# A fused GNN, Mamba and mixture-of-experts kernel: blocks chosen by the eight largest keys, logits folded by the transposing product, sums written as integers

## The chip, the cores and the metric

One core of one Trainium2 chip. The metric is the device time of one execution in microseconds (us); the time before is the median of three runs. The trace is that of one profiled execution with its own time.

## The reference

8192 rows of 128 channels pass a graph convolution and a Mamba block, then a feed-forward layer in which each row is sent to one of eight experts:

```
h = relu(adj @ layernorm(x) @ gcn_w + gcn_b); h = layernorm(h) * ln_g + ln_b
xc, z = split(h @ w_in); u = silu(conv4(xc) + conv_b); dt, B, C = from u @ w_xp
hst = exp(dt * A) * hst + dt * B * u          # a scan over the 8192 rows, 16 states
x = x + ((hst @ C + u * D) * silu(z)) @ w_out
H = gelu(layernorm(x) @ W1 + b1); probs = softmax(H @ Wg + bg)
e = argmax(probs); x = x + probs[e] * (H @ Wd[e] + bd[e])
```

## The kernel before

The rows are cut into 16 tiles of 512. Each engine (TensorE: PE, VectorE: DVE, ScalarE: ACT, GpSimd: POOL, SyncE: SP) runs its own hand-written program of bodies i = -2 to 15, each of 16 slots s. In body i, DVE scans the 16 states of tile i, one state in each slot (L984), with the product for the next state (L1057) and the running sum (L1027) beside it, POOL multiplies the states by C (L506), PE streams the adjacency product of tile i+2 (L1197), and the expert work of tile i-1 is strewn over the slots. The order on each engine is the order of the code; engines meet at semaphores that count finished steps.

Three small pieces of DVE work in each body belong to the experts.

- `logits_below_max` (slot 12): ACT has copied the partial logits from PSUM to `front_b` (L564), where channel 32k+e holds the part of expert e from quarter k of the hidden units; PE has transposed the four blocks of 128 columns into `ps_y` (L1175). DVE adds the four quarters (L943), adds the bias `bg` (L945), takes the largest (L948) and subtracts it (L950). `probability` (slot 14) picks the expert.
- `destinations` (slot 0, in the last body also slot 9): PE has ranked the rows of a tile by expert; DVE computes for each row its place in the bins in DRAM, as a float sum (L900), casts it (L902), masks it to an integer (L904) and moves the expert's `tail` on (L906). POOL then scatters the rows into the bins.
- `control` (slot 1 of bodies 4 to 15): of 32 candidate blocks (eight experts, four blocks each) those that are full (`has`) are numbered by a scan along the row (L843, L846); four masks of 32 say which candidate has number 1, 2, 3 and 4 (`chosen`, L848), and a product and a sum (L852, L856) give the four block starts, cast to integers (L861) and split into expert (`owner`) and row (`row_at`). SP reads those numbers into registers and loads the four blocks and the weights of their experts; PE, ACT and DVE then run the batch.

After the last tile five more batches empty the bins. Their `control` has the flag `flush`, and then also finds which rows are missing (L868 to L874). Batch 0's stands in slot 9 of body 15; those of batches 1 to 4 (`choose`) come behind the bodies. After them the dense computation of the last tile and the late batches run.

Between DVE instructions that depend on each other stands a wait on the step counters `ctrl_step`, `flush_step`, `gate_step` and `dest_step`.

Of the kernel before, what the change touches and what calls it, by code (L numbers as in the profile page):

```python
# [37 lines left out]
AX = mybir.AxisListType.X  # L38
EXP_LN_SET = "natural_log_exp_and_others"
# [11 lines left out]
def gnn_mamba_moe(nc, x_rows, x_cols, adj, vecs, consts, sel, gcn_w, w_in, w_xp, w_dt, w_out, W1, Wg, Wd, bd, out):  # L51
# [12 lines left out]
    with ExitStack() as ctx:  # L64
# [20 lines left out]
        eps_col = sb("eps_col", [P, 1])  # L85

# [56 lines left out]
        dest_f = sb("dest_f", [P, BLOCKS])  # L143
# [6 lines left out]
        turn = sb("turn", [P, PICKS, EXPERTS * PICKS])  # L150
        unit_row = sb("unit_row", [P, EXPERTS * PICKS])

        has = sb("has", [P, EXPERTS, PICKS])
        order = sb("order", [P, EXPERTS, PICKS])
# [5 lines left out]
        first_f = sb("first_f", [P, 2, PICKS])  # L160
# [73 lines left out]
        def cells(ap):  # L234
            return ap.rearrange("p b c -> p (b c)")
# [46 lines left out]
        gate_step, expo_ready, rank_done = sem("gate_step", 9), sem("expo_ready"), sem("rank_done")  # L282
        dest_step, scat_in = sem("dest_step", 6), sem("scat_in", 16 * BLOCKS)

        ctrl_step, flush_step = sem("ctrl_step", 13), sem("flush_step", 17)
# [60 lines left out]
        def _(sp):  # L346
# [36 lines left out]
            def body(i, p, adjacency, front, mamba, ffn, scatter, batch, late):  # L383
# [6 lines left out]
                for s in range(SLOTS):  # L390
# [20 lines left out]
                    if s == 9 and batch:  # L411
                        for n in range(AREAS):
                            sp.wait_ge(zero_in[n], 16 * PARTS)
                        c.wait(ctrl_step, -4, 13)
# [19 lines left out]
            def late_rows(f):  # L434
                sp.wait_ge(flush_step, 17 * f + 17)
# [24 lines left out]
        def _(pool):  # L460
# [7 lines left out]
            constant(turn[:], [[1, PICKS], [0, EXPERTS * PICKS]], 1, 0)  # L468
# [15 lines left out]
            def body(i, p, adjacency, front, mamba, ffn, scatter, batch, late):  # L484
# [3 lines left out]
                for s in range(SLOTS):  # L488
                    if late and s in OUT_SLOTS:
                        c.wait(o_ready, -5, PICKS + 1)  # L490
                    if scatter and s == 1:
                        if i - 2 < AREAS:
                            pool.wait_ge(zero_in[i - 2], 16 * PARTS)
                        c.wait(dest_step, -2, 6)
                        c.wait(xn_ready, -2, BLOCKS)
                        c.wait(id_step, -2, 1)
                    if fast and s == 10:
                        c.wait(dest_step, -1, 6)
# [32 lines left out]
        def _(act):  # L531
# [26 lines left out]
            act.wait_ge(start_a, 2)  # L558

            def logit_columns(c, front):  # L560
# [3 lines left out]
                nc.scalar.copy(front_b[:], ps_y[:, 0]).then_inc(cols_ready, 1)  # L564

            def body(i, p, adjacency, front, mamba, ffn, scatter, batch, late):
# [32 lines left out]
                for s in range(SLOTS):  # L599
# [105 lines left out]
                    if ffn and s == (7 if fast else 13):  # L705
                        c.wait(gate_step, -1, 4)
# [56 lines left out]
            c.wait(gate_step, -1, 4)  # L763
# [12 lines left out]
        def _(dve):  # L776
# [4 lines left out]
            nc.vector.memset(unit_row[:], 1.0).then_inc(start_v, 1)  # L781
            nc.vector.memset(ones[:], float(EXPERTS)).then_inc(start_v, 1)
            dve.wait_ge(start_c, 8)
# [30 lines left out]

            rest = H[0:EXPERTS, 0, 0:P]
# [8 lines left out]
            dve.wait_ge(start_v, 9)  # L824
            dve.wait_ge(part_step, 6)

            def control(c, d, r, flush):
# [3 lines left out]
                def after(n):  # L831
                    if flush:
                        dve.wait_ge(flush_step, 17 * d + n)
                    else:
# [28 lines left out]
                nc.vector.tensor_scalar(owner[:, r], row_at[:, r], EXPERTS - 1, None, ALU.bitwise_and  # L863
                                        ).then_inc(mark, 1)
                nc.vector.tensor_scalar(row_at[:, r], row_at[:, r], SPACE - 1, None, ALU.bitwise_and
                                        ).then_inc(mark, 1)
                if flush:
                    nc.vector.tensor_tensor(left[:], over_picks(tail[:]), cand[:], ALU.subtract).then_inc(mark, 1)  # L868
                    after(14)
                    nc.vector.tensor_tensor(weigh[:], chosen[:], over_turns(left[:]), ALU.mult).then_inc(mark, 1)  # L870
                    after(15)
                    nc.vector.reduce_sum(first_f[:, 1], weigh[:], AX).then_inc(mark, 1)
                    after(16)
                    nc.vector.tensor_scalar(absent[:, r - 2], first_f[:, 1], need[:, 0:1], float(1 << 30), ALU.is_lt,  # L874
# [16 lines left out]
            def destinations(c, d):  # L891
# [46 lines left out]
            def logits_below_max(c):  # L938
# [3 lines left out]
                quarters = ps_y[:, 0].rearrange("p (b k e) -> p b e k", b=BLOCKS, k=4)[:, :, 0:EXPERTS]  # L942
# [476 lines left out]
```

## Time and profile before

| | |
|---|---|
| median of three runs | 1755.98 us (1751.51 to 1758.42) |
| the profiled execution | 1760.01 us, of it 1758.2 us from the first to the last instruction (the span) |
| busy in the span | DVE 1537.9 us (87%), PE 1434.7 (82%), ACT 883.6 (50%), POOL 790.0 (45%) |
| mean granted TensorE clock | 0.911 of full speed |

The times in the rows below are us from the span's start; a bracket at the end of a row of the timeline says how long the engine stood idle before it and whose work ended that. Where one row begins 0.2 us after another, that is all the time that the first one costs its engine: an instruction's own length overlaps the next where no wait stands between them.

### The profile page before, as it was taken

What the parts mean: (1) busy time and instruction counts of PE and PEld (TensorE: products, weight loads), DVE (VectorE), ACT (ScalarE), POOL (GpSimd) and SP (SyncE); (2) the same over time, 40 slices, a digit from 0 to 9 for tenths busy, and PEclk for the clock granted to TensorE, in tenths of its full rate; (3) what the DMA queues carried; (4) which work ended last, traced back from release to release, by engine and by line L of the source; (5) the groups of instructions that cost most, each with busy time, mean ns of one, the idle gap of its engine ahead of it and who ended that gap; (6) DMA issues with size and microseconds to landing.
All of it is one profiled execution on the core that took longest, in us unless ns stands there. A gap on an engine that the chain in (4) does not pass through costs nothing. (4 is left out here: it accounts for less than half of the span.)

```text
span 1758.2 us, 15991 instructions
## 1 busy us (share of the span) xinstructions
PE 1434.7 (82%) x4051; PEld 658.9 (37%) x4051; DVE 1537.9 (87%) x2022; ACT 883.6 (50%) x1574; POOL 790.0 (45%) x396
## 2 busy tenths in 40 slices
PE   5998898888889898988989888889898894523487
PEld 2433333333334444444443434444444332221354
DVE  8057969898999999999999999999999999999842
ACT  3143445363636547473827465554737383734441
POOL 0013333443435355555545545555555454545622
PEclk9999999999999998999999999999899996665699
DMA  8888899899998888888888888878888884424350
GB/s 308 280 287 289 318 336 323 315 338 363 329 350 301 296 298 298 299 302 293 289 290 296 280 303 288 301 278 304 303 298 287 286 297 164 142 90 147 108 160 16
DMA packets 157806, 476.92 MB, mean 271 GB/s; under 512 B 19693, under 2 KB 41760, under 8 KB 157586
## 3 DMA queue, kind: packets, MB, share of 16 engines
q1 hardware_dynamic: 114098, 324.56, 52.9%
q10 hardware_dynamic: 38560, 139.48, 23.0%
q0 software_dynamic: 5056, 11.87, 1.8%
q8 instruction: 32, 0.52, 0.1%
q14 instruction: 60, 0.49, 0.1%
HBM read 445.75 MB, written 32.97 MB: 272 GB/s over the span
## 5 line engine op out<-in xcount | busy, mean ns | idle before, releaser
L1197 PE MATMUL ps_adj<-ring,nodes 128*128 128x512 f32 x2048 | 969.5, 621 | 117.1 <-DMA ring<-adj 58.5
L506 POOL TENSOR_TENSOR h_c<-hidden,bc_ring 128x1024 f32<-128x1024 f32 x256 | 602.1, 2352 | 876.4 <-DVE inject L1057 676.5
L984 DVE TENSOR_TENSOR_SCAN hidden<-decay,state,inject 128x512 f32<-128x512 f32 x512 | 627.6, 1267 | 53.8 <-ACT decay L584 30.8
L1197 PEld LDWEIGHTS ps_adj<-ring,nodes 128*128 128x128 f32 x2048 | 396.0, 199 | 642.4 <-issue 462.4
L584 ACT ACTIVATE decay<-dt_sb,negA 128x512 f32<-128x512 f32 x512 | 339.5, 712 | 9.5 <-DVE dt_sb L1011 7.5
L1057 DVE TENSOR_TENSOR inject<-dtu_sb,bc_ring 128x1024 f32<-128x1024 f32 x256 | 314.3, 1228 | 26.5 <-DMA bc_ring<-bc_dram 21.9
L577 ACT COPY state<-hidden 128x2 f32<-128x2 f32 x255 | 49.1, 193 | 496.0 <-DVE hidden L984 495.5
L1027 DVE TENSOR_TENSOR y_sum<-y_sum,h_c 128x1024 f32<-128x1024 f32 x224 | 273.6, 1221 | 7.7 <-POOL h_c L506 4.6
L480 POOL DMA_INDIRECT out<-o_sb,out_at x68 | 98.8, 1453 | 78.5 <-DVE o_sb L887 64.4
L475 POOL DMA_INDIRECT bins<-rec,dest x60 | 87.8, 1464 | 10.2 <-issue 9.3
L1124 PE MATMUL ps_f<-u_sb,wxp_sb 128*128 128x512 f32 x64 | 44.0, 825 | 42.4 <-ACT u_sb L663 42.4
L1124 PE MATMUL ps_e<-bt_sb,w_sb 128*128 128x512 f32 x112 | 61.0, 672 | 16.1 <-ACT H L714 10.7
L1124 PE MATMUL ps_e<-wd_ring,H 128*128 128x128 f32 x448 | 61.5, 293 | 14.1 <-ACT H L714 12.9
L1124 PE MATMUL ps_f<-front_a,win_sb 128*128 128x512 f32 x128 | 65.4, 637 | 4.0 <-DVE front_a L1007 2.8
L1036 DVE SCALAR_TENSOR_TENSOR u_sb<-conv_in,vec_sb,u_sb 128x512 f32<-128x512 f32 x96 | 65.0, 745 | 3.5 <-ACT u_sb L649 3.5
L1124 PEld LDWEIGHTS ps_e<-wd_ring,H 128*128 128x128 f32 x448 | 58.6, 202 | 25.1 <-ACT H L714 20.2
L1124 PE MATMUL ps_y<-wout_sb,soft 128*128 128x128 f32 x256 | 35.4, 297 | 19.2 <-DVE soft L936 19.2
L1124 PEld LDWEIGHTS ps_y<-wout_sb,soft 128*128 128x128 f32 x256 | 35.0, 213 | 28.1 <-DVE soft L936 20.8
L1007 DVE TENSOR_TENSOR front_a<-ps_f,front_b 128x512 f32<-128x512 f32 x16 | 10.9, 683 | 38.1 <-ACT front_b L619 38.1
L1124 PEld LDWEIGHTS ps_e<-bt_sb,w_sb 128*128 128x128 f32 x112 | 22.2, 212 | 51.3 <-issue 24.8
L605 ACT COPY front_a<-ps_adj 128x512 f32<-128x512 f32 x16 | 9.3, 581 | 63.4 <-PE ps_adj L1197 63.4
L1165 PE MATMUL ps_y<-const_sb,rec 128*128 128x128 f32 x64 | 11.2, 302 | 36.4 <-ACT rec L630 35.4
(203 smaller groups left out, 1271.1 us busy)
## 6 DMA issues: line engine op xcount, KB each, us to landing
ring<-adj SPq DMA_DIRECT2D x512, 512.0 KB, 5.9
bc_ring<-bc_dram ACTq DMA_DIRECT2D x256, 512.0 KB, 6.1
wd_ring<-wd_rows SPq DMA_DIRECT2D x64, 288.0 KB, 3.2
bins<-nodes SPq DMA_DIRECT2D x32, 516.0 KB, 8.0
got<-bins SPq DMA_DIRECT2D x60, 129.0 KB, 2.5
nodes<-x_rows ACTq DMA_DIRECT2D x8, 512.0 KB, 12.7
x_tile<-x_rows SPq DMA_DIRECT2D x16, 256.0 KB, 7.6
wd_rows<-Wd SPq DMA_DIRECT2D x8, 256.0 KB, 7.2
```

The lines of the kernel that those rows point to most:

```text
L475: nc.gpsimd.indirect_dma_start(out=bins.ap(), out_offset=bass.IndirectOffsetOnAxis(ap=dest[:, b:b + 1], axis=0), in_=rec[:, q, b], in_offs ...
L480: nc.gpsimd.indirect_dma_start(out=out, out_offset=bass.IndirectOffsetOnAxis(ap=out_at[:, r, j:j + 1], axis=0), in_=o_sb[:, r, j], in_offs ...
L506: nc.gpsimd.tensor_tensor(h_c[:, s % 2], hidden[:, s % 2], over_halves(bc_ring[:, s % BC_RING, 1]), ALU.mult).then_inc(hc_ready, 1)
L577: nc.scalar.copy(state[:, :, t:t + 1], hidden[:, t % 2, :, T - 1:T]).then_inc(state_ready, 1)
L584: exp = nc.scalar.activation(decay[:, t % 2, h], dt_sb[:, p if d == 0 else q, h], ACT.Exp, scale=negA[:, h, t:t + 1])
L984: scan = nc.vector.tensor_tensor_scan(hidden[:, s % 2, h], decay[:, s % 2, h], inject[:, h], state[:, h, s:s + 1], ALU.mult, ALU.add)
L1027: nc.vector.tensor_tensor(y_sum[:], y_sum[:], h_c[:, (s - 1) % 2], ALU.add).then_inc(y_step, 1)
L1036: nc.vector.scalar_tensor_tensor(out=u_sb[:, h], in0=conv_in[:, h, k:k + T], scalar=vec("conv_w", TAPS * h + k), in1=u_sb[:, h], op0=ALU.m ...
L1057: nc.vector.tensor_tensor(inject[:], dtu_sb[:], over_halves(bc_ring[:, t % BC_RING, 0]), ALU.mult).then_inc(inject_ready, 1)
L1124: last = nc.tensor.matmul(dst, stationary, moving, start=(n == 0), stop=(n == len(pairs) - 1))
L1165: last = nc.tensor.transpose(ps_y[:, 0, b * P:(b + 1) * P], xn_rows[:, q, b], ident)
L1197: last = nc.tensor.matmul(ps_adj[:, 0], nodes[:, m], ring[:, g % RING, m % GROUP], start=(m == 0), stop=(m == J - 1))
```

## The change

- `control`: a key for each candidate, 2^20 for a full block minus the candidate's start; one `max` instruction gives the eight largest keys of each row in falling order, so the smallest starts first. The fourth key is the threshold for `left`, and the first four, taken from 2^20 and written as integers, are the block starts. The scan, its mask, and in the non-flush form the four masks, their product and their sum go. The flush form makes the masks from the keys, later, and for the missing rows alone.
- `logits_below_max`: PE multiplies each block of `front_b` by a matrix `fold` [128, 8] that adds the four quarters, in place of the transpose; ACT's copy adds the bias (`Identity` with `bg_col`). DVE's two instructions for the quarters and the bias go, and the other two read PSUM.
- `destinations`: the sum writes integers, and the cast goes.
- At the start DVE makes `fold` and `bg_col` with three small instructions, and one memset and one iota go; ACT's bodies wait for them.

```diff
 def control(c, d, r, flush):
     ...
     after(2)
-    nc.vector.tensor_tensor_scan(cells(order[:]), unit_row[:], cells(has[:]), 0.0, ALU.mult, ALU.add
-                                 ).then_inc(mark, 1)
+    nc.vector.scalar_tensor_tensor(out=key[:], in0=has[:], scalar=float(BASE), in1=cand[:],
+                                   op0=ALU.mult, op1=ALU.subtract).then_inc(mark, 1)
     after(3)
-    nc.vector.tensor_tensor(order[:], order[:], has[:], ALU.mult).then_inc(mark, 1)
+    nc.vector.max(best[:], cells(key[:])).then_inc(mark, 1)
     after(4)
-    nc.vector.tensor_tensor(chosen[:], over_turns(order[:]), turn[:], ALU.is_equal).then_inc(mark, 1)
-    nc.vector.scalar_tensor_tensor(out=left[:], in0=order[:], scalar=float(PICKS), in1=has[:],
-                                   op0=ALU.is_le, op1=ALU.mult).then_inc(mark, 1)
+    nc.vector.tensor_scalar(left[:], key[:], best[:, PICKS - 1:PICKS], None, ALU.is_ge).then_inc(mark, 1)
+    nc.vector.tensor_scalar(row_at[:, r], best[:, 0:PICKS], -1.0, float(BASE), ALU.mult, ALU.add
+                            ).then_inc(mark, 1)
     after(5)
-    nc.vector.tensor_tensor(weigh[:], chosen[:], over_turns(cand[:]), ALU.mult).then_inc(mark, 1)
+    nc.vector.reduce_sum(taken[:], left[:], AX).then_inc(mark, 1)
     after(6)
-    nc.vector.reduce_sum(taken[:], left[:], AX).then_inc(mark, 1)
+    nc.vector.tensor_scalar(owner[:, r], row_at[:, r], EXPERTS - 1, None, ALU.bitwise_and
+                            ).then_inc(mark, 1)
     after(7)
-    nc.vector.reduce_sum(first_f[:, 0], weigh[:], AX).then_inc(mark, 1)
-    after(8)
     nc.vector.scalar_tensor_tensor(out=head[:], ...)
-    after(9)
-    nc.vector.tensor_copy(row_at[:, r], first_f[:, 0]).then_inc(mark, 1)
-    after(11)
-    nc.vector.tensor_scalar(owner[:, r], ...)
     nc.vector.tensor_scalar(row_at[:, r], row_at[:, r], SPACE - 1, None, ALU.bitwise_and
                             ).then_inc(mark, 1)
     if flush:
         nc.vector.tensor_tensor(left[:], over_picks(tail[:]), cand[:], ALU.subtract).then_inc(mark, 1)
+        nc.vector.tensor_tensor(chosen[:], over_turns(key[:]), best[:, 0:PICKS]..., ALU.is_equal).then_inc(mark, 1)
         ...
 def destinations(c, d):
     ...
-    nc.vector.reduce_sum(dest_f[:], place[:], AX).then_inc(dest_step, 1)
+    nc.vector.reduce_sum(dest[:], place[:], AX).then_inc(dest_step, 1)
     c.wait(dest_step, d, 3)
-    nc.vector.tensor_copy(dest[:], dest_f[:]).then_inc(dest_step, 1)
-    c.wait(dest_step, d, 4)
 def logits_below_max(c):
     ...
-    nc.vector.reduce_sum(logit[:], quarters, AX).then_inc(gate_step, 1)
+    nc.vector.reduce_max(top[:, 0], sums_of, AX).then_inc(gate_step, 1)
     c.wait(gate_step, -1, 1)
-    nc.vector.tensor_tensor(logit[:], logit[:], over_blocks(vec("bg", 0, EXPERTS)), ALU.add
+    nc.vector.tensor_tensor(logit[:], sums_of, over_experts(top[:, 0]), ALU.subtract
                             ).then_inc(gate_step, 1)
-    c.wait(gate_step, -1, 2)
-    nc.vector.reduce_max(top[:, 0], logit[:], AX).then_inc(gate_step, 1)
-    c.wait(gate_step, -1, 3)
-    nc.vector.tensor_tensor(logit[:], logit[:], over_experts(top[:, 0]), ALU.subtract
-                            ).then_inc(gate_step, 1)
 def logit_columns(c, front):                      # ACT
-    nc.scalar.copy(front_b[:], ps_y[:, 0]).then_inc(cols_ready, 1)
+    nc.scalar.activation(front_b[:], ps_y[:, 0], ACT.Identity, bias=bg_col[:, 0:1]).then_inc(cols_ready, 1)
 def logits():                                     # PE
-    last = nc.tensor.transpose(ps_y[:, 0, b * P:(b + 1) * P], front_b[:, b * P:(b + 1) * P], ident)
+    last = product(ps_y[:, 0, b * EXPERTS:(b + 1) * EXPERTS],
+                   [(front_b[:, b * P:(b + 1) * P], fold[:])])
 # DVE, at the start
+nc.vector.reduce_sum(fold[:], ident.rearrange("p (k e) -> p e k", k=4)[:, 0:EXPERTS], AX).then_inc(start_v, 1)
+nc.vector.tensor_tensor(expo[:, 0], ident[:, 0:EXPERTS], vec("bg", 0, EXPERTS), ALU.mult).then_inc(start_v, 1)
+dve.wait_ge(start_v, 10)
+nc.vector.reduce_sum(bg_col[:], expo[:, 0], AX).then_inc(start_v, 1)
```

DVE's program in slot 1 of a body before, from the test for full blocks to the masked row numbers:

```order
L839 SCALAR_TENSOR_TENSOR has<-cand,tail 128x32
L843 SCALAR_TENSOR_TENSOR order<-unit_row,has 128x32
L846 TENSOR_TENSOR order<-order,has 128x32
L848 TENSOR_TENSOR chosen<-order,turn 128x128
L849 SCALAR_TENSOR_TENSOR left<-order,has 128x32
L852 TENSOR_TENSOR weigh<-chosen,cand 128x128
L854 TENSOR_REDUCE taken<-left 128x8
L856 TENSOR_REDUCE first_f<-weigh 128x4
L858 SCALAR_TENSOR_TENSOR head<-taken,head 128x8
L861 CAST row_at<-first_f 128x4
L863 TENSOR_SCALAR owner<-row_at 128x4
L865 TENSOR_SCALAR row_at<-row_at 128x4
```

The same stretch of the change, on DVE, in the same slot:

```order
L842 SCALAR_TENSOR_TENSOR has<-cand,tail 128x32
L846 SCALAR_TENSOR_TENSOR key<-has,cand 128x32
L849 MAX best<-key 128x8
L851 TENSOR_SCALAR left<-key,best 128x32
L852 TENSOR_SCALAR row_at<-best 128x4
L855 TENSOR_REDUCE taken<-left 128x8
L857 TENSOR_SCALAR owner<-row_at 128x4
L860 SCALAR_TENSOR_TENSOR head<-taken,head 128x8
L862 TENSOR_SCALAR row_at<-row_at 128x4
```

Twelve instructions have become nine, the three 128 elements wide among them gone, and nothing else has moved across them: `cand` still stands ahead of the piece, and the running sum and the next state's product behind it.

DVE's program around the logits of slot 12 before, between the running sum and the next scan:

```order
L1027 TENSOR_TENSOR y_sum<-y_sum,h_c 128x1024
L943 TENSOR_REDUCE logit<-ps_y 128x32
L945 TENSOR_TENSOR logit<-logit,vec_sb 128x32
L948 TENSOR_REDUCE top<-logit 128x4
L950 TENSOR_TENSOR logit<-logit,top 128x32
L1057 TENSOR_TENSOR inject<-dtu_sb,bc_ring 128x1024
```

And in the change:

```order
L1020 TENSOR_TENSOR y_sum<-y_sum,h_c 128x1024
L941 TENSOR_REDUCE top<-ps_y 128x4
L943 TENSOR_TENSOR logit<-ps_y,top 128x32
L1050 TENSOR_TENSOR inject<-dtu_sb,bc_ring 128x1024
L977 SCALAR_TENSOR_TENSOR hidden<-decay,state,inject 128x512 x2
```

Two of the four are gone, and the two that stay now take `ps_y` as their input.

## Rows read from the trace of the kernel before

**Rows 1.** Two stretches: length, busy us of each engine (instructions), clock, DMA share, GB/s

```profile
318.00:415.00 97.00, 80.60 (x202) 33.29 (x200) 89.00 (x101) 45.81 (x87) 43.71 (x20) 0.95 0.92 334
612.00:710.00 98.00, 88.49 (x252) 40.63 (x251) 94.75 (x122) 56.75 (x100) 50.36 (x24) 0.93 0.83 291
```

**Rows 2.** What DVE waited for from 552 to 1618: us, times, longest

```profile
DVE inject L1057 <- DMA bc_ring<-bc_dram: 12.9, 10, 3.4
DVE hidden L984 <- ACT decay L584: 1.8, 3, 0.8
```

**Rows 3.** What DVE waited for from 115 to 552

```profile
DVE hidden L984 <- ACT decay L584: 29.8, 9, 10.0
```

**Rows 4.** Timeline of DVE: the control of body 4, start, us, line, operation

```profile
519.27 0.17 DVE L837 TENSOR_TENSOR cand<-head,offset 128x32 f32<-128x32 f32 x1
519.47 0.19 DVE L839 SCALAR_TENSOR_TENSOR has<-cand,tail 128x32 f32<-128x32 f32 x1
...
520.40 0.18 DVE L849 SCALAR_TENSOR_TENSOR left<-order,has 128x32 f32<-128x32 f32 x1
520.51 0.29 DVE L852 TENSOR_TENSOR weigh<-chosen,cand 128x128 f32<-128x128 f32 x1
...
521.44 0.16 DVE L865 TENSOR_SCALAR row_at<-row_at 128x4 uint32<-128x4 uint32 x1
521.51 1.41 DVE L1020 SCALAR_TENSOR_TENSOR y_sum<-u_sb,vec_sb,h_c 128x512 f32<-128x512 f32 x2
```

**Rows 5.** Timeline of DVE: the logits of body 4

```profile
587.27 0.28 DVE L943 TENSOR_REDUCE logit<-ps_y 128x32 f32<-128x128 f32 x1
...
587.81 0.19 DVE L948 TENSOR_REDUCE top<-logit 128x4 f32<-128x32 f32 x1
588.03 0.19 DVE L950 TENSOR_TENSOR logit<-logit,top 128x32 f32<-128x32 f32 x1
588.14 1.23 DVE L1057 TENSOR_TENSOR inject<-dtu_sb,bc_ring 128x1024 f32<-128x1024 f32 x1
```

**Rows 6.** Timeline of DVE: destinations in body 5

```profile
610.45 0.16 DVE L896 TENSOR_TENSOR place<-ps_y,tail 128x32 f32<-128x32 f32 x1
...
611.10 0.17 DVE L902 CAST dest<-dest_f 128x4 uint32<-128x4 f32 x1
611.30 0.17 DVE L904 TENSOR_SCALAR dest<-dest 128x4 uint32<-128x4 uint32 x1
```

**Rows 7.** Timeline of DVE: the flush control of late batch 2

```profile
1672.84 0.18 DVE L837 TENSOR_TENSOR cand<-head,offset 128x32 f32<-128x32 f32 x1
...
1675.64 0.29 DVE L872 TENSOR_REDUCE first_f<-weigh 128x4 f32<-128x128 f32 x1
...
1676.10 0.15 DVE L883 TENSOR_TENSOR out_at<-got,absent 128x4 uint32<-128x4 f32 x1
```

**Rows 8.** The chain of work that ended last, one step of it

```profile
1675.96 0.24 DVE absent L874
```

**Rows 9.** Timeline of DVE: the first instruction of the bodies

```profile
84.19 0.69 DVE L1007 TENSOR_TENSOR front_a<-ps_f,front_b 128x512 f32<-128x512 f32 x1 [38.06 <-ACT front_b L619]
```

**Rows 10.** Groups by line: busy us, mean ns, idle before and what ended it

```profile
L642 ACT ACTIVATE conv_in<-ps_f,xz_bias 128x512 f32<-128x512 f32 x32 | 20.6, 685 | 6.1 <-PE ps_f L1124 5.5
L564 ACT COPY front_b<-ps_y 128x512 f32<-128x512 f32 x16 | 9.3, 579 | 15.3 <-PE ps_y L1124 15.1
L1175 PE MATMUL ps_y<-const_sb,front_b 128*128 128x128 f32 x64 | 10.2, 284 | 2.0 <-ACT front_b L564 2.0
L1131 PE MATMUL ps_y<-vec_sb,win_sb 128*128 128x1 f32 x8 | 0.9, 240 | 0.0
```

**Rows 11.** Timeline of POOL and DVE: POOL's product beside DVE

```profile
516.95 2.34 POOL L506 TENSOR_TENSOR h_c<-hidden,bc_ring 128x1024 f32<-128x1024 f32 x1 [6.69 <-issue]
...
1654.38 5.80 POOL L506 TENSOR_TENSOR h_c<-hidden,bc_ring 128x1024 f32<-128x1024 f32 x2 [2.54 <-issue]
...
1657.89 2.31 DVE L881 CAST out_at<-got 128x4 uint32<-128x4 f32 x1
```

More of the change, by code:

```diff
@@ L142, in gnn_mamba_moe @@
         dest = sb("dest", [P, BLOCKS], U32)
-        dest_f = sb("dest_f", [P, BLOCKS])
         offset = sb("offset", [P, EXPERTS, PICKS])
-        turn = sb("turn", [P, PICKS, EXPERTS * PICKS])
-        unit_row = sb("unit_row", [P, EXPERTS * PICKS])
         has = sb("has", [P, EXPERTS, PICKS])
-        order = sb("order", [P, EXPERTS, PICKS])
+        key = sb("key", [P, EXPERTS, PICKS])
+        best = sb("best", [P, 8])
         cand = sb("cand", [P, EXPERTS, PICKS])
@@ L281, in gnn_mamba_moe @@
         h_done, h_ready, logit_done = sem("h_done", 4), sem("h_ready", 4), sem("logit_done")
-        gate_step, expo_ready, rank_done = sem("gate_step", 9), sem("expo_ready"), sem("rank_done")
-        dest_step, scat_in = sem("dest_step", 6), sem("scat_in", 16 * BLOCKS)
-        ctrl_step, flush_step = sem("ctrl_step", 13), sem("flush_step", 17)
+        gate_step, expo_ready, rank_done = sem("gate_step", 7), sem("expo_ready"), sem("rank_done")
+        dest_step, scat_in = sem("dest_step", 5), sem("scat_in", 16 * BLOCKS)
+        ctrl_step, flush_step = sem("ctrl_step", 10), sem("flush_step", 15)
         row_in, wd_in, out_in = ([sem(f"{n}{r}", 8 * PICKS) for r in range(2)] for n in ("row_in", "wd_in", "out_in"))
@@ L413, in body @@
                             sp.wait_ge(zero_in[n], 16 * PARTS)
-                        c.wait(ctrl_step, -4, 13)
+                        c.wait(ctrl_step, -4, 10)
                         c.wait(scat_in, -2, 16 * BLOCKS)
@@ L493, in body @@
                             pool.wait_ge(zero_in[i - 2], 16 * PARTS)
-                        c.wait(dest_step, -2, 6)
+                        c.wait(dest_step, -2, 5)
                         c.wait(xn_ready, -2, BLOCKS)
@@ L497, in body @@
                     if fast and s == 10:
-                        c.wait(dest_step, -1, 6)
+                        c.wait(dest_step, -1, 5)
                         c.wait(xn_ready, -1, BLOCKS)
@@ L705, in body @@
                     if ffn and s == (7 if fast else 13):
-                        c.wait(gate_step, -1, 4)
+                        c.wait(gate_step, -1, 2)
                         nc.scalar.activation(expo[:], logit[:], ACT.Exp).then_inc(expo_ready, 1)
@@ L762, in _ @@
             gelu(1, (2, 3))
-            c.wait(gate_step, -1, 4)
+            c.wait(gate_step, -1, 2)
             nc.scalar.activation(expo[:], logit[:], ACT.Exp).then_inc(expo_ready, 1)
@@ L868, in control @@
                     nc.vector.tensor_tensor(left[:], over_picks(tail[:]), cand[:], ALU.subtract).then_inc(mark, 1)
-                    after(14)
[L870 to L874, printed above, removed]
+                    nc.vector.tensor_tensor(chosen[:], over_turns(key[:]), best[:, 0:PICKS].unsqueeze(2).broadcast_to(
+                        [P, PICKS, EXPERTS * PICKS]), ALU.is_equal).then_inc(mark, 1)
+                    after(12)
+                    nc.vector.tensor_tensor(weigh[:], chosen[:], over_turns(left[:]), ALU.mult).then_inc(mark, 1)
+                    after(13)
+                    nc.vector.reduce_sum(first_f[:], weigh[:], AX).then_inc(mark, 1)
+                    after(14)
+                    nc.vector.tensor_scalar(absent[:, r - 2], first_f[:], need[:, 0:1], float(1 << 30), ALU.is_lt,
                                             ALU.mult).then_inc(mark, 1)
@@ L899, in destinations @@
                 c.wait(dest_step, d, 2)
-                nc.vector.reduce_sum(dest_f[:], place[:], AX).then_inc(dest_step, 1)
+                with nc.allow_low_precision(reason="one whole number and zeros are added"):
+                    nc.vector.reduce_sum(dest[:], place[:], AX).then_inc(dest_step, 1)
                 c.wait(dest_step, d, 3)
-                nc.vector.tensor_copy(dest[:], dest_f[:]).then_inc(dest_step, 1)
-                c.wait(dest_step, d, 4)
                 nc.vector.tensor_scalar(dest[:], dest[:], SPACE - 1, None, ALU.bitwise_and
@@ L960, in probability @@
                 nc.vector.reduce_sum(top[:, 2], expo[:], AX).then_inc(gate_step, 1)
+                c.wait(gate_step, -1, 3)
+                nc.vector.reduce_max(top[:, 1], pick[:], AX).then_inc(gate_step, 1)
+                c.wait(gate_step, -1, 4)
+                nc.vector.reciprocal(prob_col[:, q], top[:, 2]).then_inc(gate_step, 1)
                 c.wait(gate_step, -1, 5)
-                nc.vector.reduce_max(top[:, 1], pick[:], AX).then_inc(gate_step, 1)
-                c.wait(gate_step, -1, 6)
-                nc.vector.reciprocal(prob_col[:, q], top[:, 2]).then_inc(gate_step, 1)
-                c.wait(gate_step, -1, 7)
                 c.wait(rank_done, -2, 1)
@@ L992, in body @@
                         destinations(c, -1)
-                        c.wait(ctrl_step, -4, 13)
+                        c.wait(ctrl_step, -4, 10)
                         control(c, 0, 2, True)
                     if batch and s == 1:
-                        c.wait(dest_step, -2, 6)
-                        c.wait(ctrl_step, -5, 13)
+                        c.wait(dest_step, -2, 5)
+                        c.wait(ctrl_step, -5, 10)
                         c.landed(row_in, -6, p)
@@ L1101, in _ @@
             probability(c, 1)
-            c.wait(gate_step, -1, 9)
+            c.wait(gate_step, -1, 7)
             nc.vector.tensor_tensor(coef[:], pick_bf[:], over_experts(prob_col[:, 1]), ALU.mult).then_inc(coef_ready, 1)
@@ L1248, in body @@
                     if fast and s == 9:
-                        c.wait(gate_step, -1, 9)
+                        c.wait(gate_step, -1, 7)
                         rank()
@@ L1274, in body @@
                     if ffn and not fast and s == 15:
-                        c.wait(gate_step, -1, 9)
+                        c.wait(gate_step, -1, 7)
                         rank()
@@ L1314, in _ @@
             c.wait(y_ready, -1, 1)
-            c.wait(dest_step, -2, 6)
+            c.wait(dest_step, -2, 5)
             residual_product()
```

25 lines of the change are left out of this document (12 added, 13 removed).

## The prediction

> **What bounds the kernel now.** I read the stretches first. In a middle body of 98 us DVE works 94.75 us and PE 88.49 [rows 1]; since PE's busy share says little of what it waits for, I then asked for DVE's waits. Between 552 and 1618 us, a stretch of 1066 us, its two longest waits come to 12.9 and 1.8 us in all [rows 2]: from body 4 to body 15 there is nearly always a DVE instruction running, so a microsecond of DVE work left out there is a microsecond of the kernel, as long as the others keep up. In bodies 1 to 3 it is otherwise. DVE waited 29.8 us for ACT's decays between 115 and 552 [rows 3], with 89.00 us busy in 97 and the DMA engines 0.92 busy, against 0.83 in the middle [rows 1]; there the adjacency stream and what hangs on it set the pace, and shorter DVE work becomes longer waiting. Behind the bodies the chain of work that ended last runs through the flush control of batch 2 [rows 8], then SP's loads and PE's late batches.
>
> **The price of one DVE instruction** is its distance to the next one's start, not its length. From the timeline: 0.20 to 0.22 us where the next waits for it, with 32 elements wide at most [rows 4, 5]; 0.32 us where it is 128 wide (from L872 at 1675.64 to `absent` at 1675.96) [rows 7, 8]; 0.11 us where the next needs nothing of it (L849 to L852) and 0.07 for the last short one (L865 to L1020) [rows 4].
>
> **Control, slot 1.** Before: from 519.27 to 521.51, 2.24 us [rows 4]. After, in its new order: `cand` 0.20, `has` 0.22, `key` 0.22, `max` 0.23, then `left`, `row_at`, `taken`, `owner` and `head` at 0.11 each (what each waits for was started two instructions earlier), the mask 0.07: 1.49 us. It saves 0.75. No row shows `max`. From below it costs what the cheapest instruction 32 elements wide costs, 0.17 us long (`cand`), so 0.21 with its wait; from above what one 128 wide costs, 0.29 (L852) [rows 4], so 0.33. It reads 32 numbers in one pass and writes eight, which is nearest to the cheap end, so 0.23. The bounds move the saving to between 0.65 and 0.77. Twelve such controls stand in bodies 4 to 15. That of body 4, at 519, lies ahead of the last waits for the early stream, and I count it as lost: 11 x 0.75 = 8.25 us.
>
> **Logits, slot 12.** Before 587.27 to 588.14, 0.87 us [rows 5]. Two are left: the largest at 0.22 and the subtraction at 0.11 (588.03 to 588.14), 0.33. It saves 0.54; from body 4 on, 12 x 0.54 = 6.48. Both now read PSUM. `place`, which reads PSUM and is 32 wide, took 0.16 us [rows 6]; `cand`, as wide and from SBUF alone, took 0.17 [rows 4]; so PSUM adds nothing in my sum. The Trainium skill, in "VectorE: DVE Perf Modes", section "The TRN2 errata — SBUF-src ops pay a fixed extra latency per instruction", gives a VectorE instruction a fixed 58 cycles from SBUF and 120 from PSUM, which speaks against this edit: as an estimate from its 0.96 GHz, 62 cycles are 0.065 us, twice in each of 12 bodies 1.6 us, and the saving would be 16.7 in place of 18.25. The row does not agree with the page, and I follow the row.
>
> **Destinations.** The cast goes: 611.10 to 611.30, 0.20 us [rows 6]. From body 5 on there are eleven in slot 0 and one more in slot 9 of body 15: 12 x 0.20 = 2.40. That a sum writes integers costs what writing floats costs; the cast does that conversion in 0.17 us for the same four numbers, most of which every short instruction here takes.
>
> **Flush.** Before, 1672.84 to 1676.10: 3.26 us [rows 7]. After: the ten steps of above 1.49, `left` 0.11, `chosen`, `weigh` and the sum 0.32 each, `absent` 0.14: 2.70. It saves 0.56. Of the five, batch 0's stands in body 15, where DVE is the bound, and batch 2's on the last chain: 2 x 0.56 = 1.12. Batches 1, 3 and 4 are chosen beside PE's and SP's work and count nothing.
>
> **What is added elsewhere.** ACT's copy becomes an activation with a bias, 685 ns in place of 579 [rows 10], 0.11 us in a body in which ACT works 56.75 of 98 us [rows 1]. PE's four transposes took 10.2/16 = 0.64 us in a body; the nearest row of a narrow f32 product is L1131, 0.9 us for four products [rows 10], so PE gets 0.3 us more where it has 9.5 free [rows 1], and slot 12 waits for neither: DVE's row of the logits has no bracket [rows 5]. If that cover were gone, 0.4 us times 12 would take 5 of the 18. The three start instructions, some 0.5 us, stand in front of 38.06 us in which DVE has nothing to do [rows 9], and ACT's new wait ends in that same stretch. What sits behind the waits on `gate_step` and `dest_step` (ACT's exponentials, PE's ranks, POOL's scatters) is released earlier or as before; no queue gets a new instruction.
>
> **The sum.** 8.25 + 6.48 + 2.40 + 1.12 = 18.25 us off the profiled execution's own 1760.01: 1741.8. That execution is 4.0 us over the median of the runs, 1755.98, so against the median **1738 us**, 1.0% faster. In the early bodies 3 x 0.54 (logits), 3 x 0.20 (destinations) and 0.75 (control of body 4) are left out, 3.0 us.
>
> **Rivals.** *The early bodies give theirs too.* If the waits for decays there are themselves set by DVE, 3.0 us more go: 1735. For it: each such wait hangs on a chain through DVE's own instructions; against it: the DMA share of 0.92 [rows 1].
>
> *The transfers keep the pace.* DVE waits ten times for the rows of B and C, 12.9 us [rows 2]. If those land when they land, whatever DVE does, a gain made ahead of such a wait ends in it. With all of it lost the time stays at 1756, with half lost it is 1747. Against it: ACT issues these loads behind work that itself waits for DVE, the middle bodies move 291 GB/s, and the early ones 334 [rows 1].
>
> *`max` is slow.* If it makes eight passes, one for each result, 8 x 0.17 = 1.4 us [rows 4], a control costs 1.2 us more than I put down, 13 of them 15 us: 1753.
>
> *Slower: the new instructions meet POOL.* At 1657.89 a cast that else takes some 0.17 us took 2.31 and ended at 1660.20, when POOL's two products, begun at 1654.38, ended at 1660.18 [rows 11]: it stood still until POOL was done. Control gets two instructions of one tensor input, `left` and `row_at`, where it had a cast. If POOL's product still ran when they start, each control would stop for up to 2.1 us, 12 x 2.1 = 25 us against 18 gained: 1763. It decides from nine stopped controls on. Against it: in body 4 POOL's product ended at 519.29, when `cand` had just begun at 519.27 [rows 11, 4], 0.9 us ahead of `left`, and both are released by the same scan, which no edit moves. The Trainium skill, "SBUF — State Buffer", section "SBUF: two separate sides", says that such a VectorE instruction and a GpSimd one lock the port pair that they share, and whichever starts first holds it to its end. The trace agrees at that one place.
>
> That the change doesn't do what it says is excluded by the order of instructions, which shows the shorter pieces.
>
> **How the numbers follow.** Forecast 0.62, early bodies too 0.16, transfers 0.12, slow `max` 0.05, POOL 0.05. The likeliest one's own range is 1732 to 1743: the bounds of `max` (13 x 0.10 us, or 0.02 the other way) and some 4 us for the spread of the runs, 1751.5 to 1758.4. The range of 8 in 10 goes from 1731, the early bodies' 1735 less that spread, to 1749, which takes in transfers that keep somewhat over half of the gain. About 0.5%, 8.8 us, is what a measurement here can tell from none, so the line is at 1747. Faster: forecast and early bodies 0.78 and a third of the transfers' case, 0.82. Same: the rest of the transfers and the slow `max`, 0.13. Slower: 0.05.
>
> **What would show it.** Right, if the timeline shows controls of about 1.5 us with a `max` of about 0.2, logits of 0.33, destinations 0.2 shorter, and a body in the middle 1.5 us shorter, with DVE's waits between bodies 4 and 15 still near 15 us. Wrong: if those waits have grown by what the pieces lost (transfers), if `max` is near 1 us, if `left` or `row_at` lasts over 1 us beside POOL's product, or if the logits wait for PE.

## The result, and the profile after

| | before | after |
|---|---|---|
| median of the runs (lowest to highest, 4 each) | 1756.37 us (1751.51 to 1758.42) | 1739.16 us (1736.85 to 1739.99) |
| ratio, 95% interval | | 0.9909 [0.9888, 0.9929] |
| span of the profiled execution | 1758.2 us | 1735.0 us |
| DVE busy, mean clock | 1537.9 us, 0.911 | 1518.7 us, 0.923 |

The change made the kernel 17.2 us, 0.9%, faster; 1738 had been forecast. The pieces first. The timeline of DVE in the kernel after, around the control of body 4, answers to [rows 4]:

```profile
512.30 0.17 DVE L840 TENSOR_TENSOR cand<-head,offset 128x32 f32<-128x32 f32 x1
...
512.95 0.19 DVE L849 MAX8 best<-key 128x8 f32<-128x32 f32 x1
513.18 0.24 DVE L851 TENSOR_SCALAR left<-key,best 128x32 f32<-128x32 f32 x1
513.33 0.16 DVE L852 TENSOR_SCALAR row_at<-best 128x4 uint32<-128x4 f32 x1
...
513.83 1.41 DVE L1013 SCALAR_TENSOR_TENSOR y_sum<-u_sb,vec_sb,h_c 128x512 f32<-128x512 f32 x2
```

From `cand` to the running sum it is 1.53 us (1.49 forecast), and `max`, which no row of before showed, is 0.23 from start to start, one pass and not eight. The same view of the logits of body 4 [rows 5] and of the destinations of body 5 [rows 6]:

```profile
576.46 0.18 DVE L941 TENSOR_REDUCE top<-ps_y 128x4 f32<-128x32 f32 x1
576.68 0.19 DVE L943 TENSOR_TENSOR logit<-ps_y,top 128x32 f32<-128x32 f32 x1
576.79 1.23 DVE L1050 TENSOR_TENSOR inject<-dtu_sb,bc_ring 128x1024 f32<-128x1024 f32 x1
...
599.09 0.16 DVE L895 TENSOR_TENSOR place<-ps_y,tail 128x32 f32<-128x32 f32 x1
...
599.51 0.19 DVE L900 TENSOR_REDUCE dest<-place 128x4 uint32<-128x32 f32 x1
599.73 0.17 DVE L902 TENSOR_SCALAR dest<-dest 128x4 uint32<-128x4 uint32 x1
...
599.89 1.21 DVE L932 TENSOR_TENSOR y_sum<-y_sum,h_c 128x1024 f32<-128x1024 f32 x1
```

The logits take 0.33 us (576.46 to 576.79), the figure of the forecast, and have no bracket: they don't wait for PE. Read from PSUM, the two instructions last 0.18 and 0.19 us, as they did from SBUF [rows 5]. The destinations take 0.80 us, and the sum that writes integers is as long as one that writes floats. But from body 5 on the control looks otherwise. POOL and DVE, control of body 7 (POOL's L478 is the scatter of the finished rows):

```profile
792.44 2.35 POOL L504 TENSOR_TENSOR h_c<-hidden,bc_ring 128x1024 f32<-128x1024 f32 x1 [4.62 <-DVE inject L1050]
...
794.67 0.17 DVE L840 TENSOR_TENSOR cand<-head,offset 128x32 f32<-128x32 f32 x1
...
794.93 1.01 POOL L478 DMA_INDIRECT out<-o_sb,out_at  x1 [0.15 <-DVE hidden L977]
...
795.54 0.40 DVE L851 TENSOR_SCALAR left<-key,best 128x32 f32<-128x32 f32 x1
795.70 0.25 DVE L852 TENSOR_SCALAR row_at<-best 128x4 uint32<-128x4 f32 x1
...
796.35 0.74 DVE L1013 SCALAR_TENSOR_TENSOR y_sum<-u_sb,vec_sb,h_c 128x512 f32<-128x512 f32 x1
```

`left` lasts 0.40 us in place of 0.24 and the control 1.68. The scatter ends at 794.93 + 1.01 = 795.94; `left` ends at 795.54 + 0.40 = 795.94 and `row_at` at 795.95. So it is in all eleven controls of bodies 5 to 15, to within 0.02 us: both instructions stand still until the scatter is done.

What did DVE wait for? The same two stretches as in [rows 2] and [rows 3], shifted to the bodies of the faster kernel (545 to 1594, then 115 to 545):

```profile
DVE inject L1050 <- DMA bc_ring<-bc_dram: 11.2, 10, 1.7
DVE hidden L977 <- ACT decay L583: 1.5, 3, 0.7
...
DVE hidden L977 <- ACT decay L583: 25.2, 7, 8.9
```

Two bodies, 2 and 5, in the view of the stretches, from one gate product to the next (they answer to [rows 1]):

```profile
316.80:412.50 95.70, 81.93 (x211) 34.40 (x209) 88.50 (x98) 45.89 (x87) 43.70 (x20) 0.96 0.96 343
601.10:694.80 93.70, 84.24 (x249) 39.55 (x248) 91.18 (x114) 54.46 (x97) 49.37 (x24) 0.95 0.84 297
```

Cut at the starts of the gate product `soft<-y_sum` (the first of body 1, of body 5, and the one behind body 15), the spans divide so. DVE's waits are its idle times of over 0.15 us, those that the timeline shows in brackets, and its work is the rest of the stretch. Each kernel was profiled twice:

| us | before | before, again | after | after, again |
|---|---|---|---|---|
| to body 1 | 212.4 | 212.6 | 214.4 | 213.7 |
| bodies 1 to 4 | 400.4 | 398.4 | 386.7 | 388.1 |
| bodies 5 to 15 | 1049.7 | 1047.9 | 1036.0 | 1041.0 |
| of these DVE's waits | 15.5 | 14.0 | 17.2 | 21.9 |
| of these DVE's work | 1034.2 | 1033.8 | 1018.8 | 1019.1 |
| behind body 15 | 95.8 | 97.0 | 97.9 | 97.3 |
| span | 1758.2 | 1755.8 | 1735.0 | 1740.1 |

In bodies 5 to 15 DVE's work fell by 15 us in both pairs, and 2 to 8 us of that came back as waits. The early bodies, from which nothing had been expected, are 10 to 14 us shorter (3.6 us less work, 7 to 10 less waiting), and the end of the program is not shorter at all. The way to body 1 is 1 to 2 us longer here, but it lies between 212.0 and 215.6 us in all the traces, so the three start instructions can't be seen in it. The sum came out near the forecast because these errors have opposite signs, which is luck.

### The profile page after: what moved, and what is told of

It is laid out like the page before. It is cut to its first block and busy times, and to the rows that moved or that the text cites. A ratio compares the mean times of both kernels' runs of the same rounds, so it can differ in the third digit from the quotient of the medians.

```text
span 1735.0 us, 16027 instructions
## 1 busy us (share of the span) xinstructions
PE 1431.1 (82%) x4115; PEld 665.0 (38%) x4115; DVE 1518.7 (88%) x1931; ACT 885.1 (51%) x1574; POOL 788.2 (45%) x395
## 5 line engine op out<-in xcount | busy, mean ns | idle before, releaser
L1050 DVE TENSOR_TENSOR inject<-dtu_sb,bc_ring 128x1024 f32<-128x1024 f32 x256 | 314.1, 1227 | 25.3 <-DMA bc_ring<-bc_dram 21.5
L478 POOL DMA_INDIRECT out<-o_sb,out_at x68 | 98.6, 1450 | 80.7 <-DVE o_sb L886 66.6
L1117 PE MATMUL ps_e<-bt_sb,w_sb 128*128 128x512 f32 x112 | 63.4, 694 | 15.4 <-ACT H L713 9.5
L1000 DVE TENSOR_TENSOR front_a<-ps_f,front_b 128x512 f32<-128x512 f32 x16 | 10.9, 682 | 38.5 <-ACT front_b L618 38.5
L1117 PEld LDWEIGHTS ps_f<-u_sb,wxp_sb 128*128 128x128 f32 x64 | 14.2, 242 | 68.8 <-ACT u_sb L662 56.5
```

The lines of the kernel that those rows point to most:

```text
L478: nc.gpsimd.indirect_dma_start(out=out, out_offset=bass.IndirectOffsetOnAxis(ap=out_at[:, r, j:j + 1], axis=0), in_=o_sb[:, r, j], in_offs ...
L1050: nc.vector.tensor_tensor(inject[:], dtu_sb[:], over_halves(bc_ring[:, t % BC_RING, 0]), ALU.mult).then_inc(inject_ready, 1)
L1117: last = nc.tensor.matmul(dst, stationary, moving, start=(n == 0), stop=(n == len(pairs) - 1))
```

## The experiments

Each ran beside the kernel before on the same chip; the ratio is to that.

**One part alone.** Three kernels have the kernel before with one of the three parts: control, logits or destinations.

> The control alone is changed; logits and destinations are as before. Theory (from body 5 on every microsecond of VectorE work is one of the kernel): a control of 1.53 us in body 4 and 1.69 after it, 0.55 us a body off the distance of the bodies from 5 on, 11 x 0.55 and two flush controls at 0.5, so 6 to 8 us faster, ratio 0.996. Rival (the transfers keep the pace): VectorE's waits between bodies 4 and 15 grow from 15 us by what the controls lost, and the time stays within 2 us of before.

> The logits alone are changed. Theory: 0.87 us becomes 0.33 in each body, 12 x 0.54, so 5 to 8 us faster, ratio 0.996. Rival that TensorE's and ScalarE's additions (0.3 and 0.1 us a body) are paid on the way: VectorE waits at the logits' first instruction, and the gain is under 3 us.

> The destinations alone are changed: the sum writes integers, the cast is gone. Theory: 1.01 us becomes 0.80, 12 x 0.2, so 2.4 us faster, ratio 0.9986, at the edge of what the timing tells; the trace shows the 0.8. Rival (the transfers keep the pace): no change.

| | median us | ratio | DVE's work, bodies 5 to 15 | its waits |
|---|---|---|---|---|
| before, beside them | 1753.26 (1753.11 beside the second control) | 1 | 1034.2 | 15.5 |
| control | 1751.36 | 0.9988 [0.9971, 1.0005] | 1026.7 | 20.0 |
| control, again | 1749.91 | 0.9978 [0.9959, 0.9998] | 1027.2 | 19.8 |
| logits | 1745.04 | 0.9957 [0.9943, 0.9972] | 1027.6 | 14.3 |
| destinations | 1753.70 | 1.0003 [0.9987, 1.0019] | 1031.1 | 21.5 |

The second run of the control was to see whether the first one's waits repeat:

> The control alone a second time. Its pieces are 6 us of work shorter from body 5 on. If the first comparison's 2 us lay in the waits of those executions, it now comes out at 3 to 7 us faster, ratio 0.996 to 0.998; if waiting takes back what the control gives, 2 us again.

The work falls as the pieces say: 7 us for the control, 6.6 for the logits, 3.1 for the destinations. The logits give it all to the kernel. In the traces of the control alone 4.3 to 4.5 us come back as waits, in that of the destinations 6.0, twice what its pieces gave, most of them for the rows of B and C. The control's 1.9 us lies where the rival had it, and the 3.2 of its second run at the foot of the 3 to 7 expected then; both have the same waits. The logits' 8.2 us is at the top of what was expected. For the destinations no change shows, and the expected 2.4 us lies at the edge of the interval. One by one the parts add up to 9 to 11 us, less than the 14 to 17 of the whole; why is not known. DVE's largest wait from 603 to 1540 us, in the second run of the control and then in the kernel with the destinations alone:

```profile
DVE inject L1050 <- DMA bc_ring<-bc_dram: 11.4, 13, 2.0
```

```profile
DVE inject L1055 <- DMA bc_ring<-bc_dram: 13.3, 11, 2.6
```

Before, the same stretch had 8.8 us of them. So the rival of the transfers seems partly true, though each figure is that of one execution.

**The scatter moved away.** In the kernel after, the scatter that stood in slot 0 goes to slot 13:

```diff
-OUT_SLOTS = (0, 10, 11, 12)
+OUT_SLOTS = (10, 11, 12, 13)
```

> The changed kernel, but POOL's first output scatter of a body is moved from slot 0 to slot 13, so that none is being written while the control of slot 1 runs. Theory (the scatter holds up the two one-input instructions of the control): `left` falls from 0.40 to 0.24 us and `row_at` from 0.25 to 0.16 in bodies 5 to 15, a control from 1.69 to 1.53, 11 x 0.16 = 1.8 us faster than the changed kernel. Rival (their length comes of something else, such as the scalar read from SBUF): `left` stays at 0.40 in these bodies.

Measured: 1737.86 us, ratio 0.9918 [0.9896, 0.9941]. POOL and DVE in the control of body 7 of this kernel:

```profile
796.07 2.35 POOL L504 TENSOR_TENSOR h_c<-hidden,bc_ring 128x1024 f32<-128x1024 f32 x1 [4.53 <-issue]
798.40 0.17 DVE L840 TENSOR_TENSOR cand<-head,offset 128x32 f32<-128x32 f32 x1
...
799.28 0.24 DVE L851 TENSOR_SCALAR left<-key,best 128x32 f32<-128x32 f32 x1
799.43 0.16 DVE L852 TENSOR_SCALAR row_at<-best 128x4 uint32<-128x4 f32 x1
```

In every body `left` lasts 0.24, and the control 1.53 but in body 5 (1.73) and in body 15, where other work stands in it: the scatter had cost 0.16 us a body, 1.7 in all, which the whole time can't show.

**Two inputs.** The same comparison as an instruction with two input tensors, with the scatter left in slot 0:

```diff
-nc.vector.tensor_scalar(left[:], key[:], best[:, PICKS - 1:PICKS], None, ALU.is_ge).then_inc(mark, 1)
+nc.vector.tensor_tensor(cells(left[:]), cells(key[:]), best[:, PICKS - 1:PICKS].broadcast_to([P, EXPERTS * PICKS]), ALU.is_ge).then_inc(mark, 1)
```

> The changed kernel with `left` made by the form with two tensor inputs, POOL's scatters where they were. If the one-input form is what meets the scatter, `left` lasts 0.19 us in all bodies, and `row_at`, which keeps its form, 0.25 in bodies 5 to 15. If anything beside the scatter is slowed, `left` still takes 0.3 us or more there.

Measured in one execution: 1737.71 us. POOL and DVE, body 6:

```profile
704.44 1.01 POOL L478 DMA_INDIRECT out<-o_sb,out_at  x1
705.05 0.19 DVE L851 TENSOR_TENSOR left<-key,best 128x32 f32<-128x32 f32 x1
705.16 0.27 DVE L852 TENSOR_SCALAR row_at<-best 128x4 uint32<-128x4 f32 x1
```

`left` now runs through the scatter in 0.19 us and ends at 705.24; `row_at`, still of the old form, ends at 705.43, with the scatter (705.45). So the form decides, but not its one input alone, and the scatter does not hold it from its start. POOL and DVE in the kernel after, in the controls of late batches 1 and 3:

```profile
1638.29 0.98 POOL L478 DMA_INDIRECT out<-o_sb,out_at  x1 [0.30 <-issue]
1639.00 0.19 DVE L849 MAX8 best<-key 128x8 f32<-128x32 f32 x1
...
1653.57 0.98 POOL L478 DMA_INDIRECT out<-o_sb,out_at  x1 [11.72 <-DVE o_sb L886]
1653.59 0.24 DVE L851 TENSOR_SCALAR left<-key,best 128x32 f32<-128x32 f32 x1
...
1654.17 0.38 DVE L862 TENSOR_SCALAR row_at<-row_at 128x4 uint32<-128x4 uint32 x1
```

`max`, which has one input too, runs close to the end of a scatter (1639.27) in its usual 0.19 us. `left` runs beside the first part of one in its usual 0.24, and only the last `tensor_scalar` of that control is held, to the scatter's end (1654.55). Counted over the fourteen traces, for instructions under 0.4 us: of `tensor_scalar` instructions and casts in SBUF, the 182 that were due to end in the last 0.30 us of a scatter were all held, and the 89 that were through by then were not; 14 that read PSUM were not held either. Of 190 others due to end there (sums, `max`, forms with two inputs) only the eleven that stood right behind a held one were. POOL's spans are rough, so the 0.30 is too.

The Trainium skill has a rule for this in "SBUF — State Buffer", section "SBUF: two separate sides": GpSimd writes the descriptors of its own DMAs through the port pair that it shares with VectorE, whichever starts first holds the pair for its whole instruction, and copies, casts and `tensor_scalar` can ask for it, a sum (`tensor_reduce`) never. The traces agree on the forms. They differ on the length: a scatter of 1.0 us holds only what runs in its last 0.30.

**More work for DVE, early and in the middle.** In the kernel after, six extra products of 128x512 behind the logits of slot 12 (4.2 us by the trace) were put into bodies 1 to 3, or 8 to 10: 13 us each time.

```diff
+if i in (1, 2, 3):
+    for n in range(6):
...
+        nc.vector.tensor_tensor(pad[:], w1_sb[:]..., win_sb[:]..., ALU.mult).then_inc(pad_step, 1)
```

> The changed kernel with six extra VectorE products of 128x512 (0.72 us each with their wait, 4.3 us together) behind the logits of bodies 1, 2 and 3. Theory of the forecast (these bodies are paced by the adjacency stream, VectorE work there lies under waits): at most half of the 13 us shows, 0 to 6 us slower than the changed kernel, and VectorE's 25 us of waits for decays before 552 us shrink. Rival (the early bodies give theirs too): 10 to 13 us slower.

> The same six products in bodies 8, 9 and 10. Theory (VectorE is the bound there): 13 us slower than the changed kernel, each of these bodies 4.3 us longer. Rival (the transfers keep the pace): under 8 us slower, with VectorE's waits for bc_ring gone in these bodies.

The kernel after ran beside them, and the kernel before was profiled once more:

> The changed kernel itself beside the kernel before on this chip. If the three parts add up as measured one by one, 9 us faster, ratio 0.995; if the first comparison holds, 16 us, 0.991. VectorE's waits between bodies 5 and 15, 17 us in the first trace, say how far they vary from one execution to the next.

> The kernel before, profiled a second time. If waits for transfers are a matter of the execution, VectorE's waits between bodies 5 and 15 lie anywhere from 14 to 22 us, as in the five other traces; if shorter work turns into waiting, they stay at 15.

| | median us | ratio | bodies 1 to 4 | bodies 5 to 15 |
|---|---|---|---|---|
| before, again | 1755.74 | 1 | 398.4 | 1047.9 |
| after, again | 1741.30 | 0.9912 [0.9890, 0.9934] | 388.1 | 1041.0 |
| more work early | 1749.56 | 0.9972 [0.9952, 0.9991] | 397.6 | 1034.9 |
| more work in the middle | 1752.62 | 0.9974 [0.9952, 0.9995] | 386.1 | 1051.4 |

The change's gain repeats, 14.4 us beside the first 17.2. Before, DVE's waits in bodies 5 to 15 came out at 14.0 us the second time, and in the six traces of kernels with all three parts in one piece they lie from 14.9 to 21.9: so 0 to 8 us of waiting came with the change, and two executions of the kernel after alone differ by 4.7.

In the middle, 11.3 of 13 us reach the kernel's time. Bodies 8 to 10 grow from 94.9, 95.4 and 94.8 us in the first trace of the kernel after to 99.3, 98.9 and 99.6, on average by 4.2 where 4.2 were put in: that DVE is the bound there is shown. Early, 8.3 of 13 us reach the kernel's time (9.5 the stretch of bodies 1 to 4). That lies between the two ranges given, nearer to the rival's. So the early bodies are for the greater part DVE's too, and the step that counted nothing there was wrong. It does not explain 10 to 14 us, though, since DVE's work fell only by 3.6 us there; the rest is waiting. How the early bodies vary by themselves is seen in the two executions of the control alone, the same kernel; the gate products of bodies 1 and 5 in the first and in the second:

```profile
211.96 1.23 DVE L929 TENSOR_TENSOR soft<-y_sum,z_sb 128x1024 f32<-128x1024 f32 x1
...
612.51 1.23 DVE L929 TENSOR_TENSOR soft<-y_sum,z_sb 128x1024 f32<-128x1024 f32 x1
```

```profile
212.99 1.23 DVE L929 TENSOR_TENSOR soft<-y_sum,z_sb 128x1024 f32<-128x1024 f32 x1
...
598.59 1.23 DVE L929 TENSOR_TENSOR soft<-y_sum,z_sb 128x1024 f32<-128x1024 f32 x1
```

400.6 us and 385.6. Against that, the five traces with all three parts in one piece and no extra work there have 386.1 to 391.0, and the two of the kernel before 398.4 and 400.4. How much of the early gain is the change's, beyond some 3 us, stays open.

**The short pieces strewn.** From the kernel with the scatter in slot 13, the control's instructions are spread over slots 1 to 7, the two of the logits stand on either side of the running sum, and those of the destinations between the long instructions of slot 0. Most now have a long instruction between themselves and the one that needs them; the last three of the destinations still follow each other:

```diff
+                    if batch and 1 <= s <= 7:
+                        next(steps, None)
-                        logits_below_max(c)
+                        lowering = logits_below_max(c)
+                        next(lowering)
...
+                        list(lowering)
```

> The changed kernel with the scatters of the fourth experiment and the small instructions strewn: the control one or two steps a slot over slots 1 to 7, the two of the logits on either side of the running sum, destinations between the large instructions of slot 0. Nothing is left out. Theory (a small instruction costs 0.11 us where its successor need not wait and 0.22 where it must): control 1.53 to about 1.0 us a body, logits 0.33 to 0.22, destinations 0.80 to 0.55, so about 0.9 us a body and 9 us faster than the changed kernel, ratio to before 0.986. Rival (the transfers take a shortening back): VectorE's waits from body 5 to 15 grow from 19 us by more than half of that, and under 4 us show.

Measured: 1733.82 us, 0.9884 [0.9857, 0.9910]. DVE's work in bodies 5 to 15 fell by another 15 us, to 1003.8, but its waits rose to 29.1, and about 5 us of the expected 9 showed: the waits took back most of it, as the rival had said, though a little more than its 4 us was left. From 603 to 1540 us its waits for B and C were:

```profile
DVE inject L1069 <- DMA bc_ring<-bc_dram: 22.9, 17, 3.2
```

They stand in slots 9 and 10. One of them, ACT and DVE (a `q` behind the engine marks the issue of a DMA):

```profile
827.71 0.33 ACTq L594 DMA_DIRECT2D bc_ring<-bc_dram  x1
...
837.30 0.36 ACTq L594 DMA_DIRECT2D bc_ring<-bc_dram  x1
837.87 1.26 ACT L668 ACTIVATE H<-ps_e,vec_sb 128x512 f32<-128x512 f32 x2
839.01 0.70 ACT L668 ACTIVATE H<-ps_y,vec_sb 128x512 f32<-128x512 f32 x1
839.73 1.28 ACT L671 ACT_TABLE_LOAD   x1
...
842.60 0.32 ACTq L594 DMA_DIRECT2D bc_ring<-bc_dram  x1
...
851.85 1.23 DVE L1069 TENSOR_TENSOR inject<-dtu_sb,bc_ring 128x1024 f32<-128x1024 f32 x1 [3.23 <-DMA bc_ring<-bc_dram]
```

ACT issues the loads from its own program. In these slots it has GELUs, table loads and copies to do first: the issue at 837.30 comes 9.6 us after the one ahead of it, where a slot lasts 6 on average, and the one at 842.60 another 5.3 later. In the kernels before and after the first of these steps is 13.0 us at the median. Counted in order, it is the load of 842.60 that DVE waits for at 851.85; DVE was ready for it 6.0 us after its issue. In bodies 5 to 14 of this kernel such a lead is 6.4 and 6.6 us at the median in slots 9 and 10, and 10.0 to 15.4 in the others. The trace of the kernel before tells the landing of 192 of its loads: they took 3.3 to 10.7 us, 6.1 at the median. A lead of 6 us is too short for about half of them. Is the load issued too late, or is the transfer too slow (9.25 us here)?

**The same loads, issued one slot earlier.** The strewn kernel with one edit:

```diff
-                    for d, t in ((0, s + 2), (1, s + 2 - SLOTS)):
+                    for d, t in ((0, s + 3), (1, s + 3 - SLOTS)):
```

> The kernel of the strewn order, with one edit: ScalarE issues each block's bc loads one slot earlier (three slots ahead of their use in place of two). In the strewn order VectorE waited 22.9 us for bc_ring between 603 and 1540 us (17 waits, the longest 3.2), nearly all in slots 9 and 10. Theory (the loads are issued too late, behind ScalarE's work of those slots): the waits for bc_ring fall under 8 us and the time lies 8 to 15 us under the strewn order's 1733.8, near 1722 (ratio to the kernel before 0.980 to 0.985). Rival (the loads take longer as more of them are under way, or ScalarE's issue now stands before its decays): the waits stay over 15 us, or waits for ScalarE's decays take their place, and the time is within 5 us of 1733.8.

Measured: **1702.91 us** (1699.7 to 1705.4, 5 runs) beside 1755.68 for the kernel before, ratio 0.9703 [0.9677, 0.9730]. Its mean granted clock and span, and DVE's longest waits from 603 to 1540 us:

```profile
core 0: 1701.1 us, clock 0.937
```

```profile
DVE hidden L989 <- issue: 0.9, 2, 0.4
DVE hidden L989 <- ACT decay L583: 0.7, 1, 0.7
```

No wait for B and C is left in bodies 5 to 15, and the shortest lead there is 10.9 us. Bodies 5 to 15 take 1008.0 us in place of 1032.9: 22.7 us less waiting (29.1 to 6.4) and 2.2 less work. Bodies 1 to 4 take 380.6 in place of 388.6. The theory of the late issue holds, at twice the expected size, since it had counted neither all waits of these bodies nor the early ones; the rival (loads that get longer, or late decays) falls. What this does not separate is a late issue from a slow load, since the longer lead covers both; the leads of slots 9 and 10 are what speaks for the issue. This kernel is 36 us faster than the changed one. The kernel before with the earlier loads alone was not run.

## Why the prediction came out right

The time was right; of its steps some were right and some were not, and that the sum lies within 1.2 us of the measured time is luck.

- **What bounds the kernel.** Right for bodies 5 to 15, where extra work showed in full. Wrong for bodies 1 to 4: the DMA share of 0.92 and DVE's 29.8 us of waits [rows 1, 3] were read as another engine's pace, but 8.3 of 13 us of extra work showed there. In part the reading holds: followed back through the trace of before, the longest of these waits (9.97 us, at 234.64) leads through ACT and PE to a load of the adjacency stream. That at 332.63 (2.29 us) leads to a copy of the front end that ACT could begin (322.95) only behind a copy of the state, which waited for DVE's own scan. The rival of the early bodies had the direction right; its 3.0 us is about the 3.6 of work that went there, not the 10 to 14 measured.
- **The price per instruction.** Right, from start to start. `max` 0.23, the logits' saving 0.54 and that of the destinations 0.21 came as worked out, and PSUM cost nothing: 0.18 and 0.19 us for the two reads. What was added elsewhere came near the forecast too: PE's products for the logits take 1.02 us a body in place of 0.64 (0.3 more expected), and ACT's copy 0.68 in place of 0.58. By the larger fixed cost for PSUM that the Trainium skill gives ("VectorE: DVE Perf Modes", section "The TRN2 errata — SBUF-src ops pay a fixed extra latency per instruction") each would have been, as an estimate, 0.065 us longer; no row shows that.
- **Control, 11 x 0.75.** Mis-sized. It saved 2.24 - 1.53 = 0.71 in body 4 but 0.55 in bodies 6 to 15, and 0.24 in body 5, where `cand` lasted 0.47 us and ended just behind POOL's product (606.43, 606.39; no run tests this): 10 x 0.55 + 0.24 = 5.7 in place of 8.25. Of what each lacks, some 0.04 is `left`, which gave 0.15 and not 0.11 to the next start; 0.16 is the scatter. The rival with POOL named the mechanism, but looked only at POOL's products, which indeed end ahead of `left`. POOL's queue had the scatter right behind them. The prediction also picked the endangered instructions by their one input, which `max` and the sums have too, and these were not held. Before, the first instruction of a form that is held was the cast near the control's end, when the scatter was over.
- **Flush.** 2.76 us (1648.83 to 1651.59) in place of 3.26 [rows 7]: 0.50 where 0.56 was forecast. On the last chain it did not show. PE behind the last gate product, in the kernel before and then in the kernel after:

```profile
1666.99 1.88 PE L1124 MATMUL ps_f<-front_a,w_sb 128*128 128x512 f32 x4
```

```profile
1641.99 2.87 PE L1117 MATMUL ps_f<-front_a,w_sb 128*128 128x512 f32 x4
```

  Its granted clock over the first 10 us behind body 15 was 0.79 before and 0.66 after (1.00 is the level of 2.4 GHz, 0.5 that of 1.2), and the same four products took 1 us more. PE had stood idle for 5.2 and 5.3 us ahead of this stretch, so that idle time does not tell the two apart. Besides, SP took 1.3 us longer from `absent` to its last load of weights. The thirteen other profiles have 96.7 to 98.1 us behind body 15, the one of the kernel before taken again too, so the 95.8 was a short one; why is not known.
- **The transfers.** Counted at 0.12 and partly true: of 15 us of DVE's work, 2 to 8 came back as waits in the two pairs, most of them for B and C. That they came at all is what the forecast's "DVE is the bound" left out: the loads are issued by ACT, and its own stretch of GELUs and table loads does not shorten when DVE's does. The step ahead of the late issues is 13.0 us before and after. That the lead was too short is shown by the last experiment.

So 18.25 us forecast stand against 17.2 measured, as terms too high (control by 2.5, waits by 2 to 8, the tail by 1 to 2) met an early part that gave 10 us or more in place of none. Most of that early part is less waiting, and its cause stays open.

## What to carry to other kernels

When the bounding engine is made shorter, look next at who issues its inputs and from how far ahead: here one slot of lead on loads that another engine issued gave 31 us on top of the strewn kernel, where all the shaved instructions had given 17. Cost short instructions from start to start, and check a cast or a `tensor_scalar` on VectorE against everything in GpSimd's queue, its DMAs included. A part whose length varies by 15 us between two executions of one kernel can't be credited to an edit of 4.

## What was unexpected of the hardware

A GpSimd scatter (1.01 us) held back two VectorE `tensor_scalar` instructions of 32 and 4 elements to its very end, but only such as ran in its last 0.30 us. It let the same comparison with two tensor inputs through, and also `max` and sums, which have one. `max` for the eight largest of 32 numbers lasts 0.19 us, no longer than a sum over as many.
